# A fused cross-attention, linear-attention and expert kernel: the shared expert of four row tiles moved from the last attention pass into the head of the expert stage, and the last slot-table writes moved ahead of the boundary between the stages

## What is computed

```
x = x + xattn(layernorm(x), ctx)         # 16 heads, 257 context rows for each sequence
x = x + attn(layernorm(x))               # causal linear attention, then a layernorm
x = x + ffn(layernorm(x))

# ffn, with x the 1024 normed rows
shared = (silu(x @ shared_wg.T) * (x @ shared_wu.T)) @ shared_wd.T
scores = sigmoid(x @ gate_w.T)                       # 64 experts
topw, topi = top_k(scores, 8);  topw /= topw.sum(-1)
routed = sum over the 8 chosen experts e of
         topw_e * (silu(x @ wg[e].T) * (x @ wu[e].T)) @ wd[e].T
out = shared + routed
```

## Time and profile before

| | |
|---|---|
| median of three runs | 1462.96 us |
| the profiled execution | 1465.62 us |
| its span, first to last instruction | 1463.8 us |
| mean granted TensorE clock | 0.963 of full speed |
| PE busy | 1339.3 us (91%) |
| DVE busy | 780.7 us (53%) |
| ACT busy | 628.1 us (43%) |
| POOL busy | 404.5 us (28%) |
| moved by DMA | 204.19 MB, mean 139 GB/s |

### The profile page before, as it was taken

One profiled execution on the slowest core, in us unless ns is written; L12 is line 12 of the kernel. 1 busy time (PEld: TensorE's weight loads), 2 busy tenths in 40 slices (PEclk: granted clock), 3 DMA queues, 4 the chain that ended last, 5 costly groups with the idle time before them and its releaser, 6 DMA issues. The chain is left out here.

```text
span 1463.8 us, 26879 instructions
## 1 busy us (share of the span) xinstructions
PE 1339.3 (91%) x7106; PEld 1031.6 (70%) x7107; DVE 780.7 (53%) x1813; ACT 628.1 (43%) x1310; POOL 404.5 (28%) x322
## 2 busy tenths in 40 slices
PE   4999999999999999999998795499999999999991
PEld 3888787888887888788885542367667776676670
DVE  3445566565655665655554344465655565656550
ACT  1444343343343333443432113266656556656550
POOL 0000030030030200300301102455665465766441
PEclk8999999999999999999998898699999999999996
DMA  8321110111110101101003002599999999999985
GB/s 317 133 96 32 31 46 16 45 31 38 37 31 30 45 15 44 31 29 39 24 1 101 30 21 109 193 290 301 339 300 317 284 319 318 351 300 306 284 222 86
DMA packets 66896, 204.19 MB, mean 139 GB/s; under 512 B 16015, under 2 KB 18319, under 8 KB 56480
## 3 DMA queue, kind: packets, MB, share of 16 engines
q1 hardware_dynamic: 42960, 159.19, 30.1%
q0 software_dynamic: 23888, 44.40, 14.3%
HBM read 176.73 MB, written 37.03 MB: 146 GB/s over the span
## 5 line engine op out<-in xcount | busy, mean ns | idle before, releaser
L1298 DVE TENSOR_TENSOR gul<-wgu,guh 128x2048 fp32r<-128x2048 f32 x71 | 162.9, 2294 | 74.9 <-ACT guh L1251 58.2
L372 POOL TENSOR_TENSOR rstd<-vep,half 128x1 f32<-128x1 f32 x32 | 17.7, 553 | 637.4 <-DVE vep L532 637.2
L1454 PE MATMUL ebank<-wd,ht 128*128 128x512 f32 x380 | 175.1, 593 | 1.0 <-ACT ht L1236 1.0
L453 ACT ACTIVATE kt<-bank,colb 128x256 f32<-128x256 f32 x128 | 60.4, 472 | 243.5 <-PE bank L823 243.3
L821 PE MATMUL bank<-ch,wkh 128*128 128x256 f32 x512 | 161.0, 314 | 1.4 <-issue 0.5
L1424 PE MATMUL ebank<-guh,xth 128*128 128x512 f32 x380 | 155.6, 409 | 4.0 <-DVE gul L1298 2.3
L1426 PE MATMUL ebank<-guh,xtl 128*128 128x512 f32 x380 | 149.2, 393 | 0.0
L1425 PE MATMUL ebank<-gul,xth 128*128 128x512 f32 x380 | 149.0, 392 | 0.0
L1176 POOL DMA_INDIRECT xg<-xn_rows,ig x95 | 127.6, 1344 | 75.6 <-issue 42.3
L823 PE MATMUL bank<-ch,wkl 128*128 128x256 f32 x512 | 144.7, 283 | 0.4 <-issue 0.4
L822 PE MATMUL bank<-cl,wkh 128*128 128x256 f32 x512 | 144.8, 283 | 0.0
(11 more groups left out here) (227 smaller groups left out, 2672.7 us busy)
## 6 DMA issues: line engine op xcount, KB each, us to landing
wgu<-in_egu SPq DMA_DIRECT2D x71, 1024.0 KB
wd<-in_edn SPq DMA_DIRECT2D x71, 512.0 KB
...
```

Of the source, the lines that this page charges most:

```text
L1298: V.tensor_tensor(gul[par][:, :, :], wgu[w][:, :, :], guh[par][:, :, :].bitcast(F32), ALU.subtract).then_inc(s_w["gu_low"], 1)
L1454: last = mm(y_ps[tile.half][:, :], tile.ht[:, c, :], wd[item.w][:, c, :], start=c == 0, stop=c == IC - 1)
```

## The change

**The shared expert is divided.** Tiles 0 to 3 stay in the ninth pass, in other slots (the new `SHARED`). Tiles 4 to 7 go to the head of stage B, as `shared_turn`, `shared_gu`, `shared_turn_h`, `shared_down` on PE with their counterparts on ACT (which now applies silu itself), DVE and SP. Their input rows are loaded ahead of the seam into buffers that both stages hold (`d.sx`, `d.sy`, laid over the keys, values and probabilities). Their weights `sgu` and `sdn` are at the same time the fourth weight buffers of stage B, so the load of the fourth expert's weights waits for them.

**The table writes.** All 8 of tile 7 are issued in stage A.

**The plan.** DVE's first part of it (up to the columns that PE turns) stands at the end of stage A. Two transfers of POOL that add zero rows stand in pass 1 of stage A and no longer in the head.

**The loads.** SP issues five weight loads ahead of the slot table in the head of stage B where there were three.

The diff, cut to what the text speaks of:

```diff
@@ -66,11 +66,9 @@
-SHARED = {0: [("xT", 0), ("xT", 1)], 1: [("gu", 0), ("gu", 1)], 3: [("hT", 0), ("hT", 1)], 5: [("down", 0)],
...
-SHARED_LAST = [("gu", 7), ("hT", 7), ("down", 7)]
+SHA = 4
+SHARED = {0: [("xT", 0), ("xT", 1)], 2: [("gu", 0)], 4: [("hT", 0)], 5: [("down", 0)], 6: [("gu", 1)], 9: [("xT", 2)], 11: [("hT", 1), ("down", 1)],
...
-        flat = [a[:, :, :].rearrange("p c s -> p (c s)") for a in (craw[0], craw[1], kt, vb[0], qb[0], qb[1], qt, xat)]
-        sx = [a[:, 0:D] for a in flat[:4]] + flat[4::2]
-        sy = [a[:, D:2 * D] for a in flat[:4]] + flat[5::2]
-        NS = len(sx)
+        flat = [a[:, :, :].rearrange("p c s -> p (c s)") for a in (craw[0], craw[1], qb[0], qt, qb[1], xat)]
+        sx, sy = [a[:, 0:D] for a in flat[:4]], [a[:, D:2 * D] for a in flat[:2]] + flat[4:]
...
             for j in range(2):
-                load_shared(j)
+                load_shared(j, sx[j], sy[j], s_sl[j])
             sp.wait_ge(s_sc, 4 * NB)
+            sp.wait_ge(s_pq, NT)
+            for j in range(2, SHA):
+                load_shared(j, sx[j], sy[j], s_sl[j])
             sp.wait_ge(s_av, NB - 1)
-            sp.wait_ge(s_pq, NT)
-            for j in range(2, NS):
-                load_shared(j)
+            sp.wait_ge(s_tr, 2 * (NB - 1))
+            for j in range(SHA, NT - 1):
+                load_shared(j, d.sx[j - SHA], d.sy[j - SHA], d.s_sl)
             body(False, True, NT, False, per_batch, on_post, on_pre, on_shared)
-            sp.wait_ge(s_ys, 16 * NT)
-            for n, j in SHARED_LAST:
-                on_shared(n, j)
-            sp.wait_ge(s_cnt, 1)
-            sp.wait_ge(s_xns, 16 * NT)
-            sp.wait_ge(s_ss, 16 * NT)
+            sp.wait_ge(s_tr, 2 * NB)
+            load_shared(NT - 1, d.sx[NT - 1 - SHA], d.sy[NT - 1 - SHA], d.s_sl)
+            sp.wait_ge(d.s_sl, 32 * (NT - SHA))
+            sp.wait_ge(s_ss, 16 * SHA)
+            sp.wait_ge(d.s_dumped[0], 16)
+            sp.wait_ge(d.s_dumped[1], 16)
...
+                    if type(t) is int and t == 0:
+                        pool.wait_ge(s_pads, 16 * (NT + 1))
+                        for acc, dumped in zip((d.acc, d.acc1), d.s_dumped):
+                            nc.gpsimd.indirect_dma_start(acc, bass.IndirectOffsetOnAxis(d.dump[:, :], 0), y[:, :], None,
+                                                         compute_op=ALU.add).then_inc(dumped, 16)
+                        for dumped in d.s_dumped:
+                            pool.wait_ge(dumped, 16)
                     nc.gpsimd.tensor_tensor(x1b[:, :], x1[:, :], rowb[:, 4, :], ALU.add).then_inc(s_x1b, 1)
                 if n == "outproj":
                     pool.wait_ge(s_pads, 16 * (NT + 1))
                     pool.sem_inc(tick, 1)
-                    for j in range(EARLY if type(t) is int and t == NT - 1 else K):
+                    for j in range(K):
...
             passes(dve, per_batch, on_post, on_pre, on_shared)
             dve.wait_ge(s_px[0], NT * PER[0] + 1)
             V.tensor_copy(d.cnt[:, :], px[0][:, 0:E]).then_inc(s_cnt, 1)
-            for n, j in SHARED_LAST:
-                on_shared(n, j)
-
+
+            dve.drain()
+            cnt, more, more2, end, start, own, picked, q4, col = d.cnt, d.more, d.more2, d.end, d.start, d.own, d.picked, d.q4, d.col
+            V.tensor_scalar(more[:, :], cnt[:, :], float(BLK), None, ALU.is_gt)
+            dve.drain()
+            a, spare = more, more2
+            for m in range(2, JB):
...
-            for e in range(2):
-                load_gu(e, e)
+            load_gu(0, 0)
             load_d(0, 0)
+            load_gu(1, 1)
+            load_d(1, 1)
+            load_gu(2, 2)
             for s, by in biased:
                 sp.sem_inc(s, by)
 
             sp.wait_ge(d.s_scat, 16 * K * NT)
             for j, r in enumerate((slice(0, 2), slice(2, NR))):
                 sp.dma_start(tg[:, r, :, :], d.table.rearrange("(r p) e w -> p r e w", p=P)[:, r, :, :]).then_inc(s_slots[j], 16)
-            load_d(1, 1)
-            load_gu(2, 2)
             load_d(2, 2)
+            sp.wait_ge(s_sgu, SHB)
             load_gu(3, 3)
+            for j in range(SHB):
+                sp.wait_ge(s_sy, j + 1)
+                sp.dma_start(d.acc[(SHA + j) * P:(SHA + j + 1) * P, :], sy[j]).then_inc(s_ss, 16)
             sp.wait_ge(s_tab, 1)
             n = count(sp)
...
-            for j in range(EARLY, K):
-                nc.gpsimd.indirect_dma_start(
-                    d.slots, bass.IndirectOffsetOnAxis(d.idx[:, j:j + 1], 0), d.entry[:, j, :], None).then_inc(d.s_scat, 16)
             for xg in tiles[1].xg:
                 nc.gpsimd.memset(xg[:, :], 0.0).then_inc(s_blank, 1)
-            pool.wait_ge(s_dump, 2)
-            for i in range(2):
-                nc.gpsimd.indirect_dma_start(sums[i], bass.IndirectOffsetOnAxis(dump[:, :], 0), tiles[1].ys[NY - 1][:, :], None,
-                                             compute_op=ALU.add).then_inc(s_added[i], 16)
             pool.wait_ge(s_blank, 2 * NX)
...
+            for j in range(2):
+                shared_xt(j)
             nc.scalar.activation(warm[:, :], cn[0:1, C_ONE:C_ONE + 1], ACT.Silu)
-            for xg in tiles[0].xg:
-                nc.scalar.activation(xg[:, :], cn[:, 0:D], ACT.Copy, scale=0.0).then_inc(s_blank, 1)
-            for i in range(2):
-                high_gu(i, i, 0)
+            for xg in tiles[0].xg[0:4]:
+                blank(xg)
+            shared_silu(0)
+            for j in range(2, SHB):
+                shared_xt(j)
+            for xg in tiles[0].xg[4:NX]:
+                blank(xg)
+            high_gu(0, 0, 0)
+            for j in range(1, SHB - 1):
+                shared_silu(j)
+            for j in range(2):
+                shared_ht(j)
+            high_gu(1, 1, 0)
+            shared_silu(SHB - 1)
+            for j in range(2, SHB):
+                shared_ht(j)
...
+
+            def shared_h(j):
+                dve.wait_ge(s_ssi, j + 1)
+                if j >= 2:
+                    dve.wait_ge(s_shT, j - 1)
+                V.tensor_tensor(tiles[j % 2].h[:, :], sgu_ps[j][:, I:2 * I], tiles[j % 2].sg[:, :], ALU.mult).then_inc(s_sh, 1)
+
+            def shared_add(j):
+                dve.wait_ge(s_sd, j + 1)
+                V.tensor_tensor(sy[j], sd_ps[j % 2][:, :], sy[j], ALU.add).then_inc(s_sy, 1)
+
+            for j in range(2):
+                shared_h(j)
             its = items0(dve, AHEAD, TAB2)
             n = count(dve)
+            shared_h(2)
...
-                halves(dve, its[i], low_x)
+            shared_h(3)
+            low_gu(0, 0, 0)
+            for j in range(2):
+                shared_add(j)
+            halves(dve, its[0], low_x)
+            for j in range(2, SHB):
+                shared_add(j)
+            low_gu(1, 1, 1)
+            halves(dve, its[1], low_x)
...
-            pe.wait_ge(s_picked, 1)
+            def shared_turn(j):
+                if j >= 2:
+                    pe.wait_ge(s_sTc, j - 1)
+                for c in range(DC):
+                    last = tr(xt_ps[j % 2][:, c * P:(c + 1) * P], sx[j][:, c * P:(c + 1) * P], ident)
+                last.then_inc(s_sT, 1)
+
+            def shared_gu(j):
+                pe.wait_ge(s_sTc, j + 1)
+                for c in range(DC):
+                    last = mm(sgu_ps[j][:, :], sxt[j][:, c, :], sgu[:, c, :], start=c == 0, stop=c == DC - 1)
+                last.then_inc(s_sgu, 1)
+
+            def shared_turn_h(j):
+                pe.wait_ge(s_sTc, SHB)
+                pe.wait_ge(s_sh, j + 1)
+                if j >= 2:
+                    pe.wait_ge(s_shTc, j - 1)
+                for c in range(IC):
+                    last = tr(xt_ps[j % 2][:, c * P:(c + 1) * P], tiles[j % 2].h[:, c * P:(c + 1) * P], ident)
+                last.then_inc(s_shT, 1)
+
+            def shared_down(j):
+                pe.wait_ge(s_shTc, j + 1)
+                if j >= 2:
+                    pe.wait_ge(s_sy, j - 1)
+                for c in range(IC):
+                    last = mm(sd_ps[j % 2][:, :], tiles[j % 2].ht[:, c, :], sdn[:, c, :], start=c == 0, stop=c == IC - 1)
+                last.then_inc(s_sd, 1)
+
+            pe.wait_ge(d.s_picked, 1)
             for f in range(4):
                 last = mm(bank[7][0:1, f * E:(f + 1) * E], col[:, f:f + 1], ident[:, 0:E], start=True, stop=True)
             last.then_inc(s_turned, 1)
+            pe.wait_ge(d.s_sl, 32 * SHB)
+            for j in range(2):
+                shared_turn(j)
+            shared_gu(0)
+            for j in range(2, SHB):
+                shared_turn(j)
+            for j in range(1, SHB):
+                shared_gu(j)
+            for j in range(2):
+                shared_turn_h(j)
+            for j in range(2):
+                shared_down(j)
             pe.wait_ge(s_tab, 1)
             its = items0(pe, 2)
             n = count(pe)
             pe.wait_ge(s_slots[1], 16)
```

(3 more changed lines are left out.)

167 lines of the change are left out of this document (93 added, 74 removed).

## The result

Four runs of the changed kernel gave 1440.63, 1440.28, 1446.20 and 1445.67 us, median 1443.15. Four of the kernel before gave a median of 1462.53. The ratio is 0.9873, 95% interval 0.9852 to 0.9893. The forecast was 1444.0 (1437 to 1453).

What follows compares the result with a forecast made beforehand. The prediction took stage B's loop as PE-bound, so only an earlier first `gate_up` pays: seam 24.6 us earlier less 5.6 for a longer head, 19.0 us gained, giving 1444.0 us, range 1437 to 1453 (8 in 10).

Steps and rivals of the forecast that it cites:

- scaling done: Ninth pass: DVE scales the attention weights ahead of the hidden product, taking 2.91 us from about 798.7, done at 801.7.
- oproj ends: Ninth pass: between 813.6, all at 2.4 GHz, and 817.8, at the old durations; middle 815.7, 10.4 us earlier.
- x1T behind oproj: Ninth pass: one gu now stands ahead instead of down, two xT and a gu; gain 2.6 us.
- seam behind the slots: Between stages: POOL begins 0.83 us behind the slots, eight table writes take 9.85 us, the barrier half a microsecond.
- seam: Border of stages A and B: at 882.1, 24.6 us earlier; wrong if not at 879 to 886.
- head: Seam to first `gate_up`: PE's order is the path, 37.1 us instead of 31.5, giving back 5.6; ends 33 and 43.
- have some 4 us left: At the seam: last two downs, stores, tile 7's row load and plan lie beside POOL's writes with that slack.
- the rival of slow gathers: Head: gathers land in 8 us, or silu and hidden products hold PE; price 5 to 11 us, longer-head chance 0.16.
- The slot table: Head: its load stands behind 4.2 MB instead of 2.6, lands at about 16 us from the seam, wanted at 21.6.
- The loop: Stage B: forecast moves it whole, 525.6 us to the end; rival: later weight loads cost 12 to 19 us, chance 0.06.
- The clock: Rival: 1.2 GHz throughout the head cancels the gain, low ninth-pass products add 10 or more: 1463 to 1475, chance 0.06.
- the rule that the prediction set beside it: Head: each wait throttles PE anew, so bursts begin at half rate; last two downs low, 3 us above the sum.

Runs made afterwards that it cites:

- again32: The changed kernel with an AND on the register value of the expert stage's waits that count second halves, tables kept at 32 bits: 1446.33 us.
- late_writes: Against the changed kernel with 16-bit item tables, five of tile 7's eight table writes moved back to the start of stage B: 1572.25 us, 0.3 below that base.
- plan_behind: Against the changed kernel with 16-bit item tables, the first part of DVE's plan moved back to the start of stage B: 1582.3 us, 9.8 above that base.
- all_three32: Against again32: last two shared downs ahead of pos, fourth head down in its own bank, low split ahead of DVE's shared adds: 1439.21 us, 7.1 below.
- gu_twice32: Against again32, the fourth shared gate_up of the head done twice: 1450.43 us, 4.1 above.
- bare_head32: Against again32, the head's whole share of the shared expert left out: 1438.78 us, 7.6 below.
- downs_first32: Against again32, shared downs 2 and 3 of the ninth pass's last step put ahead of the position matmul: 1447.68 us, 1.3 above, intervals overlapping.

## Why the prediction was right, and where it was not

| step | forecast | profiled, changed | again32 |
|---|---|---|---|
| scaling done | 801.7 | 799.6 | 798.9 |
| oproj ends | 815.7 (813.6-817.8) | 813.2 | 817.0 |
| x1T behind oproj | 4.3 | 4.2 | 4.2 |
| outproj starts to x3T | 13.4 | 12.5 | 13.1 |
| x3T to pos | 5.7 | 5.7 | 5.7 |
| slots ready | 870.9 | 867.4 | 872.9 |
| seam behind the slots | 11.2 | 9.2 | 9.5 |
| seam | 882.1 | 876.6 | 882.4 |
| head | 37.1 | 37.0 | 37.4 |
| to the end | 525.6 | 525.3 | 525.0 |

**The ninth pass.** The steps behind oproj came out within a microsecond. The one that swings is the end of oproj: in the profiled execution at the early end of its range, where everything behind the first gu runs at the upper clock, in `again32` near its late end. The forecast took the middle without knowing that both happen.

**The seam** was forecast for the wrong reason. POOL's writes were taken as what is late next; `late_writes` shows that they hold nothing. DVE's plan and SP's wait for tile 7's rows do, within half a microsecond of each other (`plan_behind`). The step that failed is the sum of POOL's issues as the seam's term: it was 2.0 us too large (11.2 for 9.2). POOL did end 10.7 us behind the slots, as summed, but the barrier didn't wait for it. Nor did the things beside it "have some 4 us left": the plan ended 1.9 us ahead of POOL. The prediction laid the last two downs, the adds and stores, and the plan side by side, and they stand in a row: the downs took 5.84 us (3.6 forecast), DVE's second add follows them at 870.91, and only behind it come the plan (871.82 to 876.24) and the load of the rows. That the real and the supposed term lie so close is luck. The bound that the prediction set for itself, a seam at 879 to 886, is missed by the profiled execution and met by `again32`.

**The head** is right to 0.1 us, but by luck: 3.8 us gained and 3.7 lost cancel. Three gu 10.46 us (10.8 forecast), the first down 18.4 from the seam (21.2 forecast), the last hT, at 899.81, 23.2 from it (27.0). PE had the upper clock sooner than I counted (the first gu took 3.83 us, not 5.3) and fewer bare waits: 3.8 us to the good. The first gu is no constant: in `all_three32` it took 5.29. What gave it back was the end: 1.6 us behind the adds on DVE, 1.0 for downs at the lower clock, and 3.5 instead of 2.7 for the register reads, which began only behind DVE's last add. `gu_twice32` and `bare_head32` show that PE's chain is what the head is made of, so the rival of slow gathers fell: the first three landed 3.3 to 3.5 us after their issue, and item 0's rows were there when PE wanted them. The slot table, behind the five loads, landed some 15 us behind the seam (16 forecast), ahead of the 18.4 at which DVE read it; in `bare_head32`, with nothing else to do, DVE waited for it.

**The loop** moved as a whole. That rival would have cost 12 to 19 us; 525.3 and 525.6 leave nothing for it.

**The clock** didn't bring the loss that would have made the kernel slower: 0.91 in the head after 0.50, 0.89 in the pass after 0.86. But the rule that the prediction set beside it (the Trainium skill, "TensorE: Matmul & The Clock Gate", "HAM oscillation — how this bites in real kernels") agrees for the last two downs in the changed kernel, though not in `all_three32`. By it the head would have been 3 us longer than the sum; measured are 1.0 in the changed kernel, 2.4, 2.3 and 2.9 in three variants (6.14, 5.95 and 6.62 us for 3.70), and nothing in `all_three32` (3.67). The first gu behind the seam lost 0.2 us in the changed kernel and 1.7 in `all_three32` (3.83 and 5.29 us; at the upper clock 3.60). And it decides what small edits are worth here (`downs_first32`).

**The sum.** 24.6 - 5.6 = 19.0 was forecast, and 30.1 - 5.5 + 0.3 = 24.9 measured between the profiled executions. Between the medians it is 19.4. The agreement with the median is partly luck: an execution with the gap at L610 has the forecast seam, one without it has an earlier one.
